# Turning the 128 x 1024 matrix C: identity products on TensorE, or 32 x 32 blocks on VectorE and transfers within SBUF

## The chip, the cores and the metric

The kernel runs on one core of a Trainium2 chip. The metric is the device time of one execution in microseconds (us); lower is better. All data are fp32. The traces were taken by the hardware profiler; times in a trace count from the start of its span.

## What is computed

Two layers, each a residual with a dense weight and a low-rank part that is picked per batch by a label:

```python
def _L0(x, labeler_index, W, lora_A, lora_B_w):
    base  = jnp.einsum('bsi,oi->bso', x, W)
    low   = jnp.einsum('bsi,bir->bsr', x, lora_A[labeler_index])       # rank 32, 5 labels
    return base + jnp.einsum('bsr,or->bso', low, lora_B_w) * 0.5

def _L1(x, adapter_mapping, W, b, lora_As, lora_Bs):
    base_out = jnp.einsum('bti,oi->bto', x, W) + b
    lora_h   = jnp.einsum('bti,bir->btr', x, lora_As[adapter_mapping]) # rank 16, 32 slots
    return base_out + jnp.einsum('btr,bro->bto', lora_h, lora_Bs[adapter_mapping]) * 2.0

x = x + _L0(x, itok_B_0_2, L0_W, L0_lora_A, L0_lora_B_w)      # x: (8, 256, 1024)
x = x + _L1(x, itok_B_0_23, L1_W, L1_b, L1_lora_As, L1_lora_Bs)
```

## The kernel before

**The dense part.** The two layers are folded into one matrix M = (I + W0)(I + W1), up to transposes. Stage 0 computes M, stages 1 and 2 multiply it by the two halves of x. Each stage is one multiplication of 2 x 2 blocks, done with seven block products instead of eight (`ORDER`), so there are 21 products, numbered n = 0 to 20; product 7 is the first of stage 1. Each operand is split into a high and a low part (`split`, L232): ScalarE writes the rounded high part (L234, tiles `arXh`, `brh`), VectorE the rest (L235, `arXl`, `brl`). A product is four output tiles (`tile(n, i)`, one PSUM bank each) of four steps k, and a step is three matmuls of 512 columns, so a product is 48 matmuls. `kept` (L333) takes a finished tile out of PSUM. Odd products read the ring half `ar1`, even ones `ar0`.

**The low-rank part and C.** What layer 1's down projections see is x after layer 0, so the kernel forms C, the gathered down projections (8 batches x 16 ranks = 128 rows) times I + W0, 128 rows by 1024 features. `across` makes C in two halves of 512 features, each in one PSUM bank: half 0 in bank `ps6` (done during product 1), half 1 in bank `ps7` (done at "sx", during product 3). The products of stages 1 and 2 need C with features in the partitions, as tile `ctile[128 features, 8, 128 rows]`, so each 128 x 128 block of C is turned. Before the change `ct_split` (L513) splits the half into `cth` (ScalarE, L515) and `ctl` (VectorE, L516), and `ct_turn` (L519) does eight matmuls of 128 columns with the identity `eye_r` (four blocks, high and low part), then ScalarE copies the bank to `ctile` (L526). Half 0 is turned between the first two tiles of product 2, half 1 before the last tile of product 3.

**Who reads ctile.** `load_a0(c)` (L628) splits 32 of the 128 rows for chunk c into `astk` (L234 on ScalarE, L235 on VectorE). `low_a` (L669) multiplies `astk` by x from the end of product 7 on; `low_rows` (L680) takes the result out into `pstk` (two ScalarE copies, a VectorE CAST at L688 and a VectorE subtraction at L689), and `low_f` (L695) is the next matmul on that bank, 18 matmuls after `low_a` ends. `pstk10` is the first of those tiles for chunk 1, in product 10.

**Memory.** `ct`, `a1hl`, `b0s` and others lie in the same bytes as the `keep` tiles of stages 1 and 2. Before, the first writers of those (L354, L364, L282 into `keep_w`) wait for the second turn, "tr 1".

**What sets the order.** The program is recorded as jobs with an assumed duration, and `rehearse` (L61) simulates five queues. PE keeps the order in which the code is written. On ScalarE, VectorE, GpSimd and the DMA-issuing SyncE a job is picked by the earliest start and then by its due time, which is worked backwards from the PE matmul that needs it. So a change of one job can move others on these four engines. Every engine runs its list in order, and a wait holds all that stands behind it. All DMAs are issued by SyncE (`transfer`, L190), one after another.

Of the kernel before, what the change touches and what calls it, by code (L numbers as in the profile page):

```python
# [6 lines left out]
ALU = mybir.AluOpType  # L7
# [114 lines left out]
def bass_blocks(nc, x, labels, w0, a0, b0, w1, bias, a1, b1, out):  # L122
    ctx = ExitStack()
    with ctx:
        def sb(name, shape, dt, where=None):
            return (where or ctx).enter_context(nc.sbuf_tensor(name, shape, dt))

        def sem(name):
            return ctx.enter_context(nc.semaphore(name))
# [12 lines left out]
        b0s = sb("b0s", [128, NK, 4, R], F32R, small)  # L142
        ct = [sb(f"ct{j}", [128, 512], F32R, small) for j in "hl"]
        b0raw = sb("b0raw", [128, NK, R], F32, small)
# [16 lines left out]
        eye = sb("eye", [128, 128], F32)  # L161
        eye_r = sb("eye_r", [128, 128], F32R)
        bias_t = sb("bias_t", [128, NO], F32)
# [6 lines left out]
        s_raw = [sem(f"s_raw{n}") for n in range(NRAW)]  # L170
        s_a1, s_b0, s_lab, s_bias = sem("s_a1"), sem("s_b0"), sem("s_lab"), sem("s_bias")
        counts, tokens, label = {}, {}, {}
        plan = Plan()

        def tk(*name):
            return tokens.setdefault(name, Token())
# [4 lines left out]
        def act(waits, emit, token, took):  # L181
            plan.put("act", waits, emit, token, took)

        def dve(waits, emit, token, took):
            plan.put("dve", waits, emit, token, took)
# [19 lines left out]
        def pe(out_ap, lhs, rhs, start, waits=(), name=None):  # L205
            n = 1
            for s in rhs.shape[1:]:
                n *= s
            plan.put("pe", waits, (out_ap, lhs, rhs, start), tk(*name) if name else Token(), max(n / 2400 + 0.0133, 0.107))
            plan.jobs[-1].named = bool(name)  # L210

        def take(bank):
            return bank_free.pop(bank, [])
# [7 lines left out]
            eye[:, :], ones[:, :], [[-1, 128]], ALU.is_equal, 0.0, base=0, channel_multiplier=1), tk("eye"), 0.4)  # L221
        act([tk("eye")], lambda e: e.activation(eye_r[:, :], eye[:, :], ACT.Copy), tk("eye_r"), 0.3)
        dve([], lambda e: e.memset(astk[:, :, :, 64:128].bitcast(F32), 0.0), tk("zero"), 0.9)
# [109 lines left out]
        def kept(n, i, done, half=None):  # L333
# [18 lines left out]
            if p == 0:  # L352
                spare = {0: [], 1: [tk("tr", 1)], 2: [tk("stored", 1, "s1", i, 0, 1)] if stage == 2 else []}[stage]
                act([done] + spare, lambda e: e.activation(s1, z, ACT.Copy), token, 0.65)  # L354
# [7 lines left out]
            elif p == 2:  # L362
                spare = {0: [], 1: [tk("tr", 1)], 2: [tk("stored", 1, "s5", i, 1, 1)] if stage == 2 else []}[stage]
                act([done] + spare, lambda e: e.activation(s5, z, ACT.Copy), token, 0.65)  # L364
# [17 lines left out]
            else:  # L382
# [7 lines left out]
                bank_free[bank] = [token]  # L390

        where["s1", 0], where["s5", 0], where["w", 0] = mb["11"], mb["22"], mb["12"]
        for s in (1, 2):
# [22 lines left out]
        def sum_t1(stage, groups=PAIRS):  # L416
            old = {0: lambda k: [], 1: lambda k: [tk("tr", 1)], 2: lambda k: [tk("stored", 1, "w", k, 1, 0)]}[stage]
            combine(stage, "T1", "B12", "B11", ALU.subtract, where["w", stage], old, groups)
# [93 lines left out]

        def ct_split(bank, done, half):  # L513
            spare = [tk("tr", 0)] if half else []
            act([done] + spare, lambda e: e.activation(ct[0][:, :], ps[bank][:, :], ACT.Copy), tk("ct_h", half), 0.65)  # L515
            dve([tk("ct_h", half)], lambda e: e.tensor_tensor(ct[1][:, :], ps[bank][:, :], ct[0][:, :].bitcast(F32), ALU.subtract), tk("ct_l", half), 0.72)  # L516
            bank_free[bank] = [tk("ct_l", half)]

        def ct_turn(bank, half):  # L519

            for i in range(4):
                for j in range(2):
                    pe(ps[bank][:, 128 * i:128 * i + 128], ct[j][:, 128 * i:128 * i + 128], eye_r[:, :], j == 0,
                       (take(bank) if i == 0 and j == 0 else []) + [tk("ct_h", half), tk("ct_l", half), tk("eye_r")],
                       ("tr", half) if (i, j) == (3, 1) else None)
            act([tk("tr", half)], lambda e: e.activation(  # L526
                ctile[:, 4 * half:4 * half + 4, :], ps[bank][:, :].rearrange("p (k r) -> p k r", k=4), ACT.Copy), tk("ctile", half), 0.65)
            bank_free[bank] = [tk("ctile", half)]

# [30 lines left out]
        four_rows(dtmp[2][:, :], dstk[:, 0:512], tk("sum", "d", 0), ("d", 0))  # L560
        ct_split(Y[2], tk("ct", 0, 1), 0)

# [8 lines left out]
        tile(2, 0, True)  # L571
        ct_turn(Y[2], 0)
        tile(2, 1, True)
# [12 lines left out]
        side_across((2, 3))  # L586
        ct_split(Y[3], tk("sx", 3), 1)
        tile(3, 1, True)
# [5 lines left out]
        tile(3, 2, True)  # L594
        ct_turn(Y[3], 1)
        tile(3, 3, True)
# [362 lines left out]
```

How the kernel before makes its waits and increments, by code:

```python
def wait_all(eng, waits, done):  # L115
    for t in waits:
        if done.get(t.sem, 0) < t.value:
            done[t.sem] = t.value
            eng.wait_ge(t.sem, t.value)
# [72 lines left out]
            def emit(eng):  # L192
                for i in numbers:
                    if i not in label:
                        label[i] = eng.value_load(label_t[:, i:i + 1], min_val=0, max_val=top)
                for dst, src in pairs():
                    eng.dma_start(dst, src).then_inc(s, 16)
# [683 lines left out]
        def run(eng, name, s):  # L881
            done = {}
            for job in order[name]:
                wait_all(eng, job.waits, done)
                job.emit(eng).then_inc(s, 1)
# [3 lines left out]
            @block.sync  # L889
            def _(eng):
                done = {}
                for job in order["sp"]:
                    wait_all(eng, job.waits, done)
                    job.emit(eng)
                for s in s_keep.values():
                    eng.wait_ge(s, counts[s])
# [13 lines left out]
            @block.tensor  # L910
            def _(eng):
                done = {}
                wait_all(eng, [tk("fzero")], done)
                zeros = fstk[:, 0, :]
                for i in range(WARM):
                    ins = eng.matmul(ps[7][:, :], zeros, zeros.unsqueeze(1).to_broadcast([128, 4, 128]), start=True, stop=True)
                ins.then_inc(s_pe, 1)
                for job in tensor:
                    wait_all(eng, job.waits, done)
                    out_ap, lhs, rhs, first = job.emit
```

## Time and profile before

| | |
|---|---|
| median of 3 runs | 291.45 us (291.11 to 291.81) |
| the profiled execution | 291.58 us |
| its span, first to last instruction | 289.9 us |
| PE busy | 285.6 us, 99% |
| VectorE (DVE) busy | 224.0 us, 77% |
| ScalarE (ACT) busy | 144.1 us, 50% |
| mean granted TensorE clock | 0.999 |

The profiled execution has 1.68 us outside its span. A matmul's busy time overlaps that of the next, so the pace of PE is read from the starts of matmuls, not from their durations. PE is TensorE's matmuls, PEld its weight loads, SPq the queue of SyncE that issues DMAs.

### The profile page before, as it was taken

The page shows a single profiled execution, that of the slowest core. Times are in us where ns is not written, and L with a number is a line of the kernel's source. Part 1 is how long each engine was busy: PE and PEld are TensorE (multiplying, and loading weights), DVE is VectorE, ACT ScalarE, POOL GpSimd, SP SyncE. Part 2 cuts the span into 40 slices and gives each one's busy share as a digit, 9 for nine tenths or more (in the row PEclk, how much of TensorE's full clock was granted, in tenths as well). Part 3 has the DMA queues.
Part 4 walks back from the last instruction along what each step waited for, and adds up shares of the span by engine and source line. Part 5 has one row for each costly group of instructions (what it writes and reads, how often), then busy time and mean ns, then how long its engine had stood idle before and what let it go on. Part 6 is the DMA issues. An engine that isn't in the chain of part 4 may idle for free.

```text
span 289.9 us, 3654 instructions
## 1 busy us (share of the span) xinstructions
PE 285.6 (99%) x1332; PEld 238.6 (82%) x1332; DVE 224.0 (77%) x266; ACT 144.1 (50%) x194; POOL 4.0 (1%) x13
## 2 busy tenths in 40 slices
PE   8999999999999999999999999999999999999995
PEld 5888788888888888888888888888988888888885
DVE  5967999898999989999885999838385956787400
ACT  4875457625367573836473540646565373505021
POOL 0000020000000000000000000000010000000000
PEclk9999999999999999999999999999999999999999
DMA  7959600212443010117241537330102100012222
GB/s 233 362 166 351 214 0 2 83 63 72 150 140 133 14 38 5 32 42 250 73 145 39 181 103 259 111 109 37 36 0 82 65 2 0 0 72 104 80 104 78
DMA packets 18628, 29.21 MB, mean 101 GB/s; under 512 B 2994, under 2 KB 5426, under 8 KB 18610
## 3 DMA queue, kind: packets, MB, share of 16 engines
q1 hardware_dynamic: 18610, 28.98, 29.9%
q8 instruction: 10, 0.16, 0.2%
q14 instruction: 8, 0.07, 0.1%
HBM read 20.58 MB, written 8.39 MB: 100 GB/s over the span
## 4 chain that ended last, share of the span: by engine, by line
PE 97%; DMA 1%; ACT 0%; DVE 0%; issue 0%
PE ps L921 97%; DMA w_B<-in_w 1%; ACT ar0h L234 0%; ACT brh L234 0%; DVE keep_s L735 0%; DVE w_B L441 0%
## 5 line engine op out<-in xcount | busy, mean ns | idle before, releaser
L921 PE MATMUL ps<-brh,ar0h 128*128 128x512 f32 (+1 forms) x180 | 68.9, 389 | 0.1
L921 PE MATMUL ps<-brl,ar0h 128*128 128x512 f32 (+1 forms) x180 | 68.3, 385 | 0.0
L921 PE MATMUL ps<-brh,ar0l 128*128 128x512 f32 (+1 forms) x180 | 68.2, 384 | 0.0
L234 ACT ACTIVATE brh<-w_B 128x1024 fp32r<-128x1024 f32 (+1 forms) x40 | 38.8, 969 | 57.8 <-PE ps L921 49.7
L921 PE MATMUL ps<-brh,ar1h 128*128 128x512 f32 x160 | 62.5, 391 | 0.0
L921 PE MATMUL ps<-brl,ar1h 128*128 128x512 f32 x160 | 62.4, 390 | 0.0
L921 PE MATMUL ps<-brh,ar1l 128*128 128x512 f32 x160 | 62.3, 389 | 0.0
L235 DVE TENSOR_TENSOR brl<-w_B,brh 128x1024 fp32r<-128x1024 f32 (+1 forms) x40 | 44.5, 1112 | 18.5 <-ACT brh L234 18.2
L921 PEld LDWEIGHTS ps<-brh,ar0h 128*128 128x128 f32 x180 | 34.1, 190 | 7.4 <-ACT ar0h L234 0.8
L921 PEld LDWEIGHTS ps<-brh,ar0l 128*128 128x128 f32 x180 | 33.8, 188 | 6.8
L921 PEld LDWEIGHTS ps<-brl,ar0h 128*128 128x128 f32 x180 | 33.9, 188 | 6.5
L921 PEld LDWEIGHTS ps<-brh,ar1h 128*128 128x128 f32 x160 | 30.1, 188 | 6.3 <-DVE m L343 0.3
L921 PEld LDWEIGHTS ps<-brh,ar1l 128*128 128x128 f32 x160 | 30.0, 188 | 6.3
L921 PEld LDWEIGHTS ps<-brl,ar1h 128*128 128x128 f32 x160 | 30.1, 188 | 5.9
L235 DVE TENSOR_TENSOR ar0l<-w_A,ar0h 128x1024 fp32r<-128x1024 f32 (+1 forms) x16 | 17.3, 1086 | 0.7 <-ACT ar0h L234 0.5
L345 DVE SCALAR_TENSOR_TENSOR keep_s<-ps,bias_t,keep_s 128x512 f32<-128x512 f32 x16 | 11.6, 745 | 6.9 <-PE ps L921 6.9
L234 ACT ACTIVATE ar0h<-w_A 128x1024 fp32r<-128x1024 f32 (+1 forms) x16 | 15.0, 944 | 1.5 <-DVE w_A L282 1.2
L387 ACT ACTIVATE keep_s<-ps,bias_t 128x512 f32<-128x512 f32 x7 | 4.8, 687 | 21.3 <-PE ps L921 21.3
L235 DVE TENSOR_TENSOR ar1l<-w_A,ar1h 128x1024 fp32r<-128x1024 f32 (+1 forms) x14 | 14.8, 1064 | 0.7 <-ACT ar1h L234 0.5
L282 DVE TENSOR_TENSOR w_B<-w_B 128x1024 f32<-128x1024 f32 x12 | 14.4, 1219 | 0.2
L234 ACT ACTIVATE ar1h<-w_A 128x1024 fp32r<-128x1024 f32 (+1 forms) x14 | 12.9, 927 | 0.6 <-PE ps L921 0.5
L921 PE MATMUL ps<-pstk,dstk 128*128 128x512 f32 x32 | 12.4, 389 | 0.0
(109 smaller groups left out, 348.6 us busy)
## 6 DMA issues: line engine op xcount, KB each, us to landing
w_B<-in_x SPq DMA_DIRECT2D x32, 256.0 KB, 2.9
out_z<-keep_s SPq DMA_DIRECT2D x23, 256.0 KB, 2.0
w_B<-in_w SPq DMA_DIRECT2D x16, 256.0 KB, 5.7
w_A<-in_w SPq DMA_DIRECT2D x16, 256.0 KB, 5.3
raw<-in_b SPq DMA_DIRECT2D x64, 32.0 KB, 1.7
out_z<-keep_w SPq DMA_DIRECT2D x8, 256.0 KB, 2.1
raw<-in_a SPq DMA_DIRECT2D x8, 128.0 KB, 2.8
a1raw<-in_a SPq DMA_DIRECT2D x8, 64.0 KB, 1.9
```

The costliest lines, as they stand in the source:

```text
L234: act(waits + spare, lambda e: e.activation(hi, src, ACT.Copy, scale=scale), h, 0.2 + 0.43 * wide)
L235: dve([h], lambda e: e.tensor_tensor(lo, src, hi.bitcast(F32), ALU.subtract), l, 0.15 + 0.54 * wide)
L282: lambda e, part=part, ins=ins: e.tensor_tensor(place[:, part, :], ins[0], ins[1], op),
L345: dve(waits + [tk("bias")], lambda e: e.scalar_tensor_tensor(out=dst, in0=z, scalar=bias_t[:, 4 * a + i:4 * a + i + 1], in1=other, op0=ALU ...
L387: act([done, tk("bias"), tk("stored", stage, "s1", i, 0, 0)], lambda e: e.activation(s1, z, ACT.Identity, bias=bias_t[:, 4 + i:5 + i]), to ...
L921: ins = eng.matmul(out_ap, lhs, rhs, start=first, stop=False, skip_group_check=True)
```

## The change

C is no longer split and multiplied by the identity. VectorE's transpose reads the half's PSUM bank and writes tile `ct[half]`, in which each 32 x 32 block is turned in its own place. The blocks then have to change places within the 128 partitions: SyncE issues 16 transfers from SBUF to SBUF for each half, one for each pair of source and target group of 32 partitions, of 32 partitions x 4 x 32 elements of 4 bytes. The first writers of the shared bytes now wait for both halves of `ctile` and two more tokens.

```diff
-        ct = [sb(f"ct{j}", [128, 512], F32R, small) for j in "hl"]
+        ct = [sb(f"ct{h}", [128, 512], F32, small) for h in range(2)]
-        eye_r = sb("eye_r", [128, 128], F32R)
-        act([tk("eye")], lambda e: e.activation(eye_r[:, :], eye[:, :], ACT.Copy), tk("eye_r"), 0.3)
...
+        small_done = [tk("ctile", 0), tk("ctile", 1), tk("dn", 3), tk("sum", "d2")]
...
-                spare = {0: [], 1: [tk("tr", 1)], 2: [tk("stored", 1, "s1", i, 0, 1)] if stage == 2 else []}[stage]
+                spare = {0: [], 1: small_done, 2: [tk("stored", 1, "s1", i, 0, 1)] if stage == 2 else []}[stage]
...
-        def ct_split(bank, done, half):
-            spare = [tk("tr", 0)] if half else []
-            act([done] + spare, lambda e: e.activation(ct[0][:, :], ps[bank][:, :], ACT.Copy), tk("ct_h", half), 0.65)
-            dve([tk("ct_h", half)], lambda e: e.tensor_tensor(ct[1][:, :], ps[bank][:, :], ct[0][:, :].bitcast(F32), ALU.subtract), tk("ct_l", half), 0.72)
-            bank_free[bank] = [tk("ct_l", half)]
-        def ct_turn(bank, half):
-            for i in range(4):
-                for j in range(2):
-                    pe(ps[bank][:, 128 * i:128 * i + 128], ct[j][:, 128 * i:128 * i + 128], eye_r[:, :], j == 0,
-                       (take(bank) if i == 0 and j == 0 else []) + [tk("ct_h", half), tk("ct_l", half), tk("eye_r")],
-                       ("tr", half) if (i, j) == (3, 1) else None)
-            act([tk("tr", half)], lambda e: e.activation(
-                ctile[:, 4 * half:4 * half + 4, :], ps[bank][:, :].rearrange("p (k r) -> p k r", k=4), ACT.Copy), tk("ctile", half), 0.65)
-            bank_free[bank] = [tk("ctile", half)]
+        def ct_turn(bank, done, half):
+            dve([done], lambda e: e.transpose(ct[half][:, :], ps[bank][:, :]), tk("blocks", half), 0.72)
+            bank_free[bank] = [tk("blocks", half)]
+            views = [ct[half][32 * c:32 * c + 32, :].rearrange("p (k q r) -> p k q r", k=4, q=4) for c in range(4)]
+            transfer([tk("blocks", half)], lambda: [
+                (ctile[32 * q:32 * q + 32, 4 * half:4 * half + 4, 32 * c:32 * c + 32], views[c][:, :, q, :])
+                for c in range(4) for q in range(4)], s_ct[half], tk("ctile", half), 8, count=16)
...
-        ct_split(Y[2], tk("ct", 0, 1), 0)
+        ct_turn(Y[2], tk("ct", 0, 1), 0)
-        ct_turn(Y[2], 0)
-        ct_split(Y[3], tk("sx", 3), 1)
+        ct_turn(Y[3], tk("sx", 3), 1)
-        ct_turn(Y[3], 1)
```

The change also moves instructions, since `rehearse` orders four engines anew; PE's order is the old one less the 16 identity matmuls. Three places matter below. Line numbers of the kernel after are one to nine lower for the same statement.

SyncE, from the last small load of stage 0 to the loads of x for stage 1 (`w_B<-in_x`) and of layer 1's up projections (`raw<-in_b`). Before:

```order
66 L197 DMA bias_t<-in_bias 128x8
67 L197 DMA w_B<-in_x 128x512 x12
68 L197 ISA
69 L197 DMA raw<-in_b 16x512 x4
70 L197 ISA
71 L197 DMA raw<-in_b 16x512 x4
72 L197 DMA w_B<-in_x 128x512 x4
```

And after:

```order
66 L197 DMA bias_t<-in_bias 128x8
67 L197 DMA ctile<-ct 32x4x32 x16
68 L197 DMA w_B<-in_x 128x512 x12
69 L197 DMA ctile<-ct 32x4x32 x16
70 L197 DMA w_B<-in_x 128x512 x4
71 L197 ISA
72 L197 DMA raw<-in_b 16x512 x4
```

Half 0 is issued ahead of the twelve loads of x, half 1 between them and the last four.

ScalarE, from the high parts of product 6 (`w_B21`, `w_A22`) to those of product 7 (`w_B12`, `m_11`). Before, where both splits of `ctile` stood ten instructions earlier:

```order
L663 ACTIVATE bstk0<-raw1 128x512
L663 ACTIVATE bstk0<-raw0 128x512
L506 ACTIVATE dstk<-dtmp2 32x512 x2
L234 ACTIVATE brh<-w_B12 128x1024
L234 ACTIVATE ar1h<-m_11 128x4x256
```

And after:

```order
L654 ACTIVATE bstk0<-raw1 128x512
L500 ACTIVATE dtmp0<-ps6 32x512
L233 ACTIVATE astk<-ctile 128x8x16
L233 ACTIVATE brh<-w_B12 128x1024
L233 ACTIVATE astk<-ctile 128x8x16
L233 ACTIVATE ar1h<-m_11 128x4x256
```

The first split of `ctile`, which waits for both halves' transfers, now stands directly ahead of the high parts of product 7.

VectorE, in product 10, around the rows `pstk10` that `low_f` waits for. Before:

```order
L282 TENSOR_TENSOR w_B22<-w_B22,w_B11 128x1024
L235 TENSOR_TENSOR brl<-w_B11,brh 128x1024
L235 TENSOR_TENSOR ar1l<-w_A11,ar1h 128x4x256
L688 CAST pstk10<-ps2 32x512
L235 TENSOR_TENSOR brl<-w_B11,brh 128x1024
L689 TENSOR_TENSOR pstk10<-ps2,pstk10 32x512
```

And after:

```order
L281 TENSOR_TENSOR w_B22<-w_B22,w_B11 128x1024
L234 TENSOR_TENSOR brl<-w_B11,brh 128x1024
L679 CAST pstk10<-ps2 32x512
L234 TENSOR_TENSOR ar1l<-w_A11,ar1h 128x4x256
L234 TENSOR_TENSOR brl<-w_B11,brh 128x1024
L680 TENSOR_TENSOR pstk10<-ps2,pstk10 32x512
```

Two long subtractions now stand between the CAST and the subtraction that completes `pstk10`, where one stood.

## Rows read from the trace of the kernel before

**Rows 1.** The page: busy us (share of the span), instructions; two rows in 40 slices.
```profile
PE 285.6 (99%) x1332; PEld 238.6 (82%) x1332; DVE 224.0 (77%) x266; ACT 144.1 (50%) x194; POOL 4.0 (1%) x13
PE   8999999999999999999999999999999999999995
PEclk9999999999999999999999999999999999999999
```

**Rows 2.** The chain that ended last: start us, us, what.
```profile
0.82 2.69 DMA w_B<-in_w
...
5.16 281.80 PE ps L921 x1324
...
286.99 0.42 DVE keep_s L735
```

**Rows 3.** The timeline of PE, first turn: start us, us, engine, line, operation.
```profile
40.54 0.22 PE L921 MATMUL ps<-eye_r,cth 128*128 128x128 f32 x1
...
41.38 0.45 PE L921 MATMUL ps<-brh,ar0h 128*128 128x512 f32 x1
...
44.22 0.39 PE L921 MATMUL ps<-ar0h,a1hl 128*128 128x512 f32 x1
```

**Rows 4.** The same, second turn, and the first matmuls of products 6 and 7.
```profile
66.88 0.22 PE L921 MATMUL ps<-eye_r,cth 128*128 128x128 f32 x1
...
67.72 0.45 PE L921 MATMUL ps<-brh,ar1h 128*128 128x512 f32 x1
...
70.56 0.39 PE L921 MATMUL ps<-brh,ar0h 128*128 128x512 f32 x1
...
92.32 0.39 PE L921 MATMUL ps<-brh,ar0h 128*128 128x512 f32 x1
...
103.20 0.39 PE L921 MATMUL ps<-brh,ar1h 128*128 128x512 f32 x1
```

**Rows 5.** The groups of instructions that write cth and ctl.
```profile
L515 ACT ACTIVATE cth<-ps x2: 598/599/600, 29.6 to 59.8; 128x512 fp32r<-128x512 f32 x2
L516 DVE TENSOR_TENSOR ctl<-ps,cth x2: 677/684/690, 36.5 to 60.5; 128x512 fp32r<-128x512 f32 x2
```

**Rows 6.** The timeline of VectorE near the end of product 4, and before product 7.
```profile
77.40 1.21 DVE L282 TENSOR_TENSOR w_B<-w_B 128x1024 f32<-128x1024 f32 x1
...
97.09 1.22 DVE L235 TENSOR_TENSOR ar1l<-m,ar1h 128x1024 fp32r<-128x1024 f32 x1
```

**Rows 7.** The timeline of SyncE's queue: issues of DMAs.
```profile
33.86 0.41 SPq L197 DMA_DIRECT2D bias_t<-in_bias  x1
53.21 26.24 SPq L197 DMA_DIRECT2D w_B<-in_x  x12
81.22 3.62 SPq L197 DMA_DIRECT2D raw<-in_b  x8
84.88 2.13 SPq L197 DMA_DIRECT2D w_B<-in_x  x4
```

**Rows 8.** Transfers: packets and share of 16 engines; issues, KB each, median us to landing.
```profile
q1 hardware_dynamic: 18610, 28.98, 29.9%
...
w_B<-in_x SPq DMA_DIRECT2D x32, 256.0 KB, 2.9
...
raw<-in_b SPq DMA_DIRECT2D x64, 32.0 KB, 1.7
```

**Rows 9.** The timeline of ScalarE, high part of product 7's operand.
```profile
91.24 1.06 ACT L234 ACTIVATE brh<-w_B 128x1024 fp32r<-128x1024 f32 x1 [0.61 <-PE ps L921]
```

**Rows 10.** The timeline of all engines in product 10, around pstk10.
```profile
145.42 0.40 PE L921 MATMUL ps<-brl,astk 128*128 128x256 f32 x2
...
145.53 1.22 DVE L235 TENSOR_TENSOR ar1l<-w_A,ar1h 128x1024 fp32r<-128x1024 f32 x1 [0.54 <-ACT ar1h L234]
...
146.78 0.69 DVE L688 CAST pstk<-ps 32x512 fp32r<-32x512 f32 x1
...
148.76 0.68 DVE L689 TENSOR_TENSOR pstk<-ps,pstk 32x512 fp32r<-32x512 f32 x1
...
149.67 0.30 PEld L921 LDWEIGHTS ps<-pstk,fstk 128*128 128x128 f32 x2 [0.16 <-issue]
149.77 0.40 PE L921 MATMUL ps<-pstk,fstk 128*128 128x256 f32 x2
...
150.21 0.59 ACT L686 ACTIVATE pstk<-ps 32x512 fp32r<-32x512 f32 x1 [0.69 <-PE ps L921]
```

More of the change, by code:

```diff
@@ L171, in bass_blocks @@
         s_a1, s_b0, s_lab, s_bias = sem("s_a1"), sem("s_b0"), sem("s_lab"), sem("s_bias")
+        s_ct = [sem(f"s_ct{h}") for h in range(2)]
         counts, tokens, label = {}, {}, {}
@@ L362, in kept @@
             elif p == 2:
-                spare = {0: [], 1: [tk("tr", 1)], 2: [tk("stored", 1, "s5", i, 1, 1)] if stage == 2 else []}[stage]
+                spare = {0: [], 1: small_done, 2: [tk("stored", 1, "s5", i, 1, 1)] if stage == 2 else []}[stage]
                 act([done] + spare, lambda e: e.activation(s5, z, ACT.Copy), token, 0.65)
@@ L416, in sum_t1 @@
         def sum_t1(stage, groups=PAIRS):
-            old = {0: lambda k: [], 1: lambda k: [tk("tr", 1)], 2: lambda k: [tk("stored", 1, "w", k, 1, 0)]}[stage]
+            old = {0: lambda k: [], 1: lambda k: small_done, 2: lambda k: [tk("stored", 1, "w", k, 1, 0)]}[stage]
             combine(stage, "T1", "B12", "B11", ALU.subtract, where["w", stage], old, groups)
```

## The prediction

> **What bounds the kernel now.** I read the page first. TensorE is busy for 99% of the span and full in every slice but the first and the last, at the full granted clock throughout, while VectorE has 77% and ScalarE 50% [rows 1]. The chain of waits says the same more strictly: after 5.16 us of start-up it is one piece of 281.80 us on PE with 1324 matmuls, and only the last 0.4 us are VectorE's [rows 2]. So the end is set by how many matmuls PE issues and at what pace, and anything else counts only if it makes PE wait. Next I read the pace, from starts of matmuls. Product 6 begins at 92.32 and product 7 at 103.20 [rows 4]: 48 matmuls of 512 columns in 10.88 us, 0.2267 us each. That is the yardstick for what the identity products cost. Last I looked at what stands near the new steps on VectorE, ScalarE and SyncE's queue, to find how late C may come [rows 6 to 10].
>
> **What goes from PE.** Each turn is eight matmuls of 128 columns. In the first turn they start at 40.54 and the next real product at 41.38, 0.84 us. But that product is slowed too: the twelve matmuls of its tile last until 44.22 [rows 3]. From 40.54 to 44.22 are 3.68 us, and twelve at the yardstick are 12 x 0.2267 = 2.72, so the turn costs 0.96 us. The second turn: from 66.88 to 70.56 again 3.68 us with twelve product matmuls in it [rows 4], again 0.96. Both stand in the unbroken PE piece, so both are on the path: 2 x 0.96 = **1.92 us** to gain. The lower bound of the gain, if the slow tile after the turn has another cause, is 2 x 0.84 = 1.68 us.
>
> **What speaks against it in the notes.** The row shows 0.96 us for four blocks of 128 x 128 in two parts, all of it on the engine that bounds. The Trainium skill (VectorE: DVE Perf Modes, Rules for kernel authors) says to turn 128 x 128 on TensorE where PSUM may be the destination, and its table of the three transpose paths gives 390 ns on TensorE for one such block of bf16 and 311 ns on VectorE for one that is turned only within 32 x 32 blocks. By its figures the estimate for eight blocks is 3.1 us on TensorE instead of the 1.92 that the rows give, and the gain would be larger than I take. The rule looks at the engine's own time, and here the row decides.
>
> **What goes from and comes to VectorE and ScalarE.** ScalarE loses two writes of `cth` at 0.598 us [rows 5], two copies to `ctile` and `eye_r`; at 50% it gives nothing to the path. VectorE loses two subtractions of 0.684 us and gets two transposes of the same 128 x 512 from PSUM. No row shows a transpose. Nearest are the subtraction at 0.684 [rows 5] and, above, an instruction of twice the elements, 1.22 [rows 6]. A gain is excluded, since both read the same bank once at one column after another. I take 0.69, the same size. At 1.22 each, 0.5 us more stands ahead of work with some us of cover: nothing on the path.
>
> **Half 0 on SyncE.** C's first half is in PSUM by 29.6, and VectorE subtracts at 36.5 [rows 5], where the transpose stands now, so it is turned by 37.2. SyncE has nothing to issue from 34.3 to 53.21 [rows 7]. Sixteen issues fit: the eight small loads `raw<-in_b` took 3.62 us [rows 7], 0.45 us each, so 7.2 us, to about 44.5. Cost nothing; the cover is 8 us. PE's `down` on the same bank now waits for the transpose alone, earlier than before.
>
> **Half 1, the step that could bite.** All times here are on the clock of the trace; with PE 1.9 us ahead most of them move together. VectorE turns half 1 only after the subtraction that starts at 77.40 and ends at 78.6 [rows 6], although C is there at 59.8 [rows 5]. Turned by 79.3. SyncE then issues 16 transfers of 0.45 us, to 86.5. Landing takes 1.7 us for small loads and 2.9 for loads of x [rows 8], so C is complete between 88.2 and 89.4. The engines set a second limit. A transfer of 32 x 4 x 32 elements is 128 runs of 128 bytes, so a half is 2048, or 128 on each of 16 engines. The page has 18610 packets in 29.9% of 16 engines' span [rows 8]: 0.299 x 16 x 289.9 / 18610 = 0.0745 us each. 128 of these are 9.5 us, and C would be complete at 79.3 + 9.5 + 1.7 = 90.5. So the bounds are 88.2 and 90.5, and I take 89.4, as the mean packet is much larger than 128 bytes.
>
> Who waits: ScalarE's first split of `ctile` now stands directly ahead of `brh` for product 7, which ran at 91.24 and waited for PE then [rows 9]. With C by 90.5 and 0.3 us for the split, it isn't even moved. If it were, there is more cover. The last low part of product 7 was ready at 97.09 + 1.22 = 98.3 [rows 6], and PE takes it at the third step, six matmuls after 103.20 [rows 4], at 104.56: 6.2 us. VectorE's split of `ctile` stands ahead of the copy of product 5's last bank, which product 6 wants only at its last tile, 36 matmuls after 92.32: no less cover. So PE waits only if C is complete later than 91.24 + 6.2 - 0.3 = 97.1. Behind the 16 issues on SyncE stand the last four loads of x (84.88 before, about 86.6 now) and `raw<-in_b`, 81.22 before and about 88.7 now [rows 7]. The first are operands of product 8 and later; the latter's low-rank matmuls come after product 7. Both have over 10 us: nothing.
>
> **The moved VectorE step in product 10.** `low_a` for chunk 1 issues its last matmul at 145.54, the second of the pair at 145.42, and a reader starts 0.32 us after such a matmul (149.89 to 150.21) [rows 10]. Now the CAST is taken at 145.86, `ar1l` 0.72 later (146.58), `brl` 1.14 later (147.72) and the subtraction 1.26 later (148.98), against 148.76 before; it ends 0.68 later at 149.66. PE loads these weights at 149.67 and multiplies at 149.77 [rows 10], so the cover of 0.22 us is just used up. I put **0.1 us**, with 0 and 0.3 as ends. Around product 8 the same swap has over a microsecond left by the same counting.
>
> **Sum.** On the profiled execution: 291.58 - 1.92 + 0.1 = 289.76. The median of the runs is 0.13 below it, so I forecast 291.45 - 1.92 + 0.1 = 289.6 us. Its own range is 289.3 (the full gain and some noise) to 290.0 (1.68 gained and 0.3 lost).
>
> **Rivals.** (1) *VectorE hands part back.* VectorE's list is reordered over products 2 to 10, and PE now asks 1.9 us sooner. For it: the thin 0.22 us in product 10, and others I may have missed. Against: PE's piece of the chain is unbroken [rows 2], and the covers are microseconds elsewhere. Two or three such stalls of 0.3 us give 290.3.
>
> (2) *The gain does not show.* If some supplier runs on its own time from 67 us on, PE just waits 1.9 us once. For it: loads of x are issued one after another, 32 issues more. Against: all products' operands wait for PE's release of the ring, and so move with it. It would give 291.4.
>
> (3) *The transfers are slow, and it is slower than before.* The mechanism is half 1's small packets holding ScalarE's queue ahead of product 7's high parts. It decides from a completion at 97.1, so from 17.8 us for the half, 1.1 us per transfer. If a 128-byte packet took twice the mean of the page, 0.149 us, 128 of them take 19.1 us and C is complete at 79.3 + 19.1 + 2.9 = 101.3. PE waits 4.2 us, and the time is 291.45 - 1.92 + 4.2 = 293.7 us. For it: such a packet is not in the trace. Against: the mean packet is 1.56 KB and takes 0.0745 us, and a smaller one should not take longer. The Trainium skill (DMA: Bandwidth & Descriptors, Specifications) puts the least transfer for line rate at 512 bytes and says that below it the engine reads, modifies and writes; this rival is that rule as a doubling. That the bytes per packet are small is certain; that the doubled time passes the cover is not.
>
> **How the numbers follow.** Forecast 0.72; VectorE hands back 0.12; no gain shows 0.09; slow transfers 0.07. A measurement of this kernel can tell about 0.2%, 0.58 us. Below 290.87 lie the forecast and the first rival: faster 0.84. Within 0.2% the second: 0.09. Slower 0.07. The range must leave out no more than 0.2: from 289.2 it reaches past the first rival, to 290.8, which holds 0.84.
>
> **What would show it.** PE should have 1316 matmuls, and go from tile to tile at 0.2267 us where the turns stood, with the starts of product 7 at about 101.3. Sixteen issues of 0.45 us should follow the transpose near 77.5 (79.3 less 1.9), with completion near 87.5, and ScalarE's split of `ctile` should wait for DMA by less than 2 us. A gap before the first `pstk`,`fstk` matmul of product 10 would show the small loss. The prediction is wrong if PE's rows show a wait for ScalarE or VectorE at the start of product 7, if one issue takes a microsecond, or if a transpose takes several.

## The result

| | before | after |
|---|---|---|
| median of 8 runs each, same chip | 291.48 us (291.11 to 292.03) | 290.50 us (290.29 to 291.31) |
| ratio to before, with its 95% interval | | 0.9968 (0.9957 to 0.998) |
| the profiled execution | 291.58 us | 290.38 us |
| its span | 289.9 us | 288.7 us |

The change makes the kernel 0.98 us faster, 0.3%. The forecast was 289.6 us, a gain of 1.85 us. The sign is right and 290.5 lies in the range, but half of the gain is missing. Five more runs of the changed kernel beside before on another chip gave 290.55 us and 0.9961 (0.9948 to 0.9973), so the missing half is no accident of one chip.

The page of after, in the same form as [rows 1]:

```profile
PE 283.7 (98%) x1316; PEld 236.3 (82%) x1316; DVE 223.3 (77%) x266; ACT 140.4 (49%) x189; POOL 2.9 (1%) x13
PE   7999999999999999999999999999999999999995
```

TensorE has 16 matmuls fewer, as it should, and seems as full as before. Nothing on this page says where 0.9 us went. The chain that ended last does (start us, us, what; before it was one unbroken piece of PE, [rows 2]):

```profile
34.80 79.32 PE ps L912 x356
114.19 1.06 ACT ar1h L233
...
119.62 0.69 DVE pstk L680
120.56 165.20 PE ps L912 x786
```

The chain leaves PE at 114.19, in product 8, and comes back at 120.56 by a VectorE instruction, L680, the subtraction that completes the rows `pstk`. So somewhere near 120 us PE waited for VectorE, which it didn't before.

**The bookkeeping by starts of matmuls.** The cleanest way to see where time comes and goes is to put the same matmul of both kernels side by side. The timeline of PE, before, at the last product matmul ahead of the first turn and at the tile in product 8 that takes `pstk` (start us, us, engine, line, operation):

```profile
40.32 0.39 PE L921 MATMUL ps<-brh,ar0l 128*128 128x512 f32 x1
...
121.81 0.39 PE L921 MATMUL ps<-brh,ar0l 128*128 128x512 f32 x1
122.04 0.40 PE L921 MATMUL ps<-pstk,fstk 128*128 128x256 f32 x2
```

And after, at the turns' places, then at the same tile, then at its fellow in product 10:

```profile
40.14 0.39 PE L912 MATMUL ps<-brh,ar0l 128*128 128x512 f32 x1
40.37 0.39 PE L912 MATMUL ps<-brh,ar0h 128*128 128x512 f32 x1
...
65.75 0.39 PE L912 MATMUL ps<-brh,ar1h 128*128 128x512 f32 x1
...
119.73 0.39 PE L912 MATMUL ps<-brh,ar0l 128*128 128x512 f32 x1
120.56 0.48 PE L912 MATMUL ps<-pstk,fstk 128*128 128x256 f32 x2 [0.44 <-DVE pstk L680]
120.87 0.40 PE L912 MATMUL ps<-brh,ar0h 128*128 128x512 f32 x1
...
148.12 0.39 PE L912 MATMUL ps<-brh,ar0l 128*128 128x512 f32 x1
148.49 0.48 PE L912 MATMUL ps<-pstk,fstk 128*128 128x256 f32 x2
148.80 0.39 PE L912 MATMUL ps<-brh,ar0h 128*128 128x512 f32 x1
```

The product tile behind the first turn started at 41.38 before [rows 3] and starts at 40.37 now, 1.01 earlier; that behind the second at 67.72 [rows 4] against 65.75, 1.97 earlier. Just ahead of `pstk` the two stand at 121.81 and 119.73: 2.08 earlier. Not all of that is the turns': the last product matmul ahead of the first turn stands at 40.32 and 40.14, 0.18 earlier already, since PE's small waits before 36 us came out shorter in this execution. The two turns together brought 2.08 - 0.18 = 1.90. Then comes the step from 119.73 to 120.56, 0.83 us where before had 0.23. That is 0.60 lost, and the next matmul starts 0.31 later instead of 0.23, 0.08 more. In product 10 the same two steps are 0.37 and 0.31 where before had 0.23 (149.54 to 149.77) and 0.24: 0.21 more. 2.08 - 0.68 - 0.21 = 1.19, and the spans differ by 1.2. Nothing else on the path moved. Without the 0.18 it would be 1.01, and the medians differ by 0.98.

The idle time printed beside the matmul, 0.44, is smaller than the 0.60 by the starts, since a matmul's busy time overlaps the next one's. The gap is read from starts.

### The profile page after: what moved, and what is told of

Read it like the earlier page. It is cut to its first block, busy times and chain, and to the rows that moved or that the text cites. A ratio compares the mean times of both kernels' runs of the same rounds, so it can differ in the third digit from the quotient of the medians.

```text
span 288.7 us, 3652 instructions
## 1 busy us (share of the span) xinstructions
PE 283.7 (98%) x1316; PEld 236.3 (82%) x1316; DVE 223.3 (77%) x266; ACT 140.4 (49%) x189; POOL 2.9 (1%) x13
## 2 busy tenths in 40 slices
DMA packets 23236, 29.74 MB, mean 103 GB/s; under 512 B 7602, under 2 KB 10034, under 8 KB 23218
## 3 DMA queue, kind: packets, MB, share of 16 engines
q1 hardware_dynamic: 23218, 29.51, 31.3%
## 4 chain that ended last, share of the span: by engine, by line
PE 85%; SPq 7%; DMA 2%; ACT 2%; DVE 2%; issue 1%; DVEq 0%; ACTq 0%
PE ps L912 85%; SPq L197 6%; DMA w_A<-in_w 2%; SPq L195 1%; ACT ar1h L233 1%; DVE w_A L281 0%; DVE brl L234 0%; DVE ar0l L234 0%; ACT brh L233 0%; ACT astk L233 0%; DVE pstk L680 0%; DVE m L342 0%; ACT pstk L678 0%; ACT keep_s L353 0%; ACT pstk L677 0%
## 5 line engine op out<-in xcount | busy, mean ns | idle before, releaser
L344 DVE SCALAR_TENSOR_TENSOR keep_s<-ps,bias_t,keep_s 128x512 f32<-128x512 f32 x16 | 11.6, 747 | 6.7 <-PE ps L912 6.6
```

The lines of the kernel that those rows point to most:

```text
L344: dve(waits + [tk("bias")], lambda e: e.scalar_tensor_tensor(out=dst, in0=z, scalar=bias_t[:, 4 * a + i:4 * a + i + 1], in1=other, op0=ALU ...
```

## Why VectorE was late at 119.62: reading back

Two things had changed for VectorE, and both lie ahead of that subtraction. First the order. These are the rows of VectorE before, in product 8:

```profile
118.63 0.69 DVE L688 CAST pstk<-ps 32x512 fp32r<-32x512 f32 x1
119.47 0.68 DVE L689 TENSOR_TENSOR pstk<-ps,pstk 32x512 fp32r<-32x512 f32 x1 [0.16 <-ACT pstk L687]
```

And after:

```profile
117.64 0.69 DVE L679 CAST pstk<-ps 32x512 fp32r<-32x512 f32 x1
118.36 1.22 DVE L234 TENSOR_TENSOR brl<-keep_w,brh 128x1024 fp32r<-128x1024 f32 x1
119.62 0.68 DVE L680 TENSOR_TENSOR pstk<-ps,pstk 32x512 fp32r<-32x512 f32 x1
```

A long subtraction of 1.22 us, a low part for product 9, now stands between the CAST and the step that PE waits for. It is the swap that the prediction costed in product 10. Second, VectorE had come late to this place. The queue of SyncE in after, against [rows 7], and behind it what waits for it on ScalarE and VectorE:

```profile
37.32 10.43 SPq L197 DMA_DIRECT2D ctile<-ct  x16
52.55 27.48 SPq L197 DMA_DIRECT2D w_B<-in_x  x12
80.08 10.25 SPq L197 DMA_DIRECT2D ctile<-ct  x16
90.37 2.02 SPq L197 DMA_DIRECT2D w_B<-in_x  x4
```

```profile
91.63 0.31 ACT L233 ACTIVATE astk<-ctile 128x128 fp32r<-128x128 f32 x1 [4.18 <-DMA ctile<-ct]
...
91.97 0.29 DVE L234 TENSOR_TENSOR astk<-ctile,astk 128x128 fp32r<-128x128 f32 x1 [2.98 <-ACT astk L233]
```

Sixteen issues take 10.25 us, 0.64 each, not 7.2. They also begin late, at 80.08 and not near 77.5. VectorE shows why:

```profile
76.84 0.69 DVE L342 TENSOR_TENSOR m<-ps,m 128x512 f32<-128x512 f32 x1 [0.49 <-PE ps L912]
77.44 1.22 DVE L281 TENSOR_TENSOR w_B<-w_B 128x1024 f32<-128x1024 f32 x1
78.58 0.71 DVE L516 STREAM_TRANSPOSE ct<-ps 128x512 f32<-128x512 f32 x1
```

The subtraction `w_B<-w_B` ahead of the transpose starts at 77.44, and in before at 77.40 [rows 6]: it didn't come earlier with PE, since in the new order it stands behind a copy of a bank that waits for PE, which in before ran behind it, at 78.92. And on SyncE the last two of the twelve loads of x, for which this subtraction makes room, are issued ahead of half 1, until 80.03. So C is complete at 91.6, 1.3 us after the last issue ends, ScalarE's first split of `ctile` waits 4.18 us and VectorE's 2.98 us behind it. From 91.97 to 119.62, over 27 us, VectorE has no wait in its rows: it works off what queued up. In before it still had small waits there, 0.32 us at the low part ahead of the CAST among them. So the 2.98 us are partly still there 27 us later; the experiments show 1.09 of them.

A number that helps from here on is the **cover** of `pstk` in product 8. In after the subtraction starts at 119.62 and PE's matmul at 120.56, 0.94 later, and PE wanted to start it at 119.73 + 0.23 = 119.96. The cover is what is left between the moment at which the subtraction should start at the latest (PE's wanted start less 0.94) and the start it has. In before it is 122.04 - 0.94 - 119.47 = 1.63 us, in after 119.96 - 0.94 - 119.62 = -0.60: the gap.

## The experiments

**The theory**: the identity products were worth the full 1.9 us, and about 0.6 to 0.7 came back in product 8, by the swap and by the late C together. **The rivals**: the products were worth less than was read; the new order alone costs it; the slow 128-byte packets do. All kernels are the changed one or the one before with the edit shown. `shift(lane, job, ahead_of)` takes one job out of an engine's finished list and puts it ahead of another; `("B", 1, 9, 2)` is the low part of product 9's second operand, second half, and `("p", 1, 0, c)` the subtraction that completes `pstk` of chunk c.

**1. The products alone (e_no_turn).** The kernel before, with its 16 identity matmuls left out and all else in its old order. C isn't turned here: ScalarE copies it to `ctile` as it is, once the low part is written.

```diff
         order, tensor = plan.rehearse(5.0)
+        tensor = [job for job in tensor if job.emit[2].tensor.name != eye_r.name]
...
+        for half in range(2):
+            tk("tr", half).sem, tk("tr", half).value = s_dve, tk("ct_l", half).value
```

> The kernel before with the 16 identity matmuls taken off PE and nothing else changed: ScalarE copies C to ctile unturned, so C is not turned here and the low-rank part of layer 1 is computed from the wrong layout. It prices the first term alone. By the starts of matmuls the turns cost 2 x 0.96: 291.5 - 1.9 = 289.6 us. If the slower pace of the twelve matmuls behind a turn has another cause, only 2 x 0.84 goes: 289.8 us. If PE only waits elsewhere for what it gains, it stays near 290.5.

Measured: 289.76 us against 291.66, ratio 0.9935 (0.992 to 0.9951). That is 1.90 us for the products, against 1.92 by the prediction's count of [rows 3, 4], and no gap at `pstk`. The first rival falls: the term of the sum was right, the loss comes from the new parts.

**2. The order alone (e_before_swap).** The kernel before, with VectorE's list changed as in after: in product 8 the long subtraction ahead of the completing one, in product 10 the CAST ahead of `ar1l`.

```diff
+        shift("dve", ("B", 1, 9, 2), ("p", 1, 0, 0))
+        shift("dve", ("p", 3, 0, 1), ("A", 1, 11, 0))
```

> The kernel before, identity products and all, with VectorE's list changed only where the kernel after has it changed around pstk: in product 8 one brl ahead of the subtraction of pstk00, in product 10 the CAST ahead of ar1l. Theory L: in the kernel before VectorE is not behind, the subtraction of pstk00 ends 1.15 us later at 121.3 and PE wants it at 121.9, so no gap there; at most 0.2 us in product 10. Time 291.5 to 291.7 us. Rival O: PE loses 0.6 us at pstk00 and 0.2 at pstk10, 292.3 us.

Measured: 291.67 us against 291.66, ratio 1.0002 (0.999 to 1.0014). In product 8 the step stays at 0.22 us (121.73 to 121.95). The subtraction starts at 120.52, so the cover went from 1.63 to 121.95 - 0.94 - 120.52 = 0.49 us, and it holds. The swap alone isn't enough. In product 10 the gap is there: 149.46 to 149.83, 0.37 us, just as in after, so that small one is the order's alone. Its 0.2 us are too few to be seen in the medians.

**3. C early (e_early).** The changed kernel, with half 1's transpose and its 16 transfers moved ahead, ahead of a low part of product 4 and of loads of x.

```diff
+        shift("dve", ("blocks", 1), ("A", 1, 4, 2))
+        shift("sp", ("ctile", 1), ("f", 1, "B12", 0))
```

> The kernel after, with two moves and nothing else: VectorE's transpose of half 1 stands ahead of the last low part of product 4 (about 60 us) and SyncE's 16 transfers ahead of the loads of w_B11, so C is complete some 20 us earlier. The two moved steps of pstk in products 8 and 10 stay as in the kernel after. Theory L (late C): the kernel after loses 0.6 us at the first pstk,fstk matmul (119.73 to 120.56) because C is complete only at about 91.6, ScalarE waits 4.2 us for it, VectorE 3.0 us for ScalarE, and VectorE is still behind in product 8. Then here ScalarE's wait for C is gone, the subtraction of pstk00 ends near 119.2, PE goes through at 0.23 us, and the time is 290.5 - 0.7 = 289.8 us. Rival O (order alone): the swap on VectorE's list costs the 0.6 us by itself; then PE's gap stays at 0.8 us between starts and the time stays at 290.5.

Measured: 289.73 us against 291.66, ratio 0.9933 (0.9919 to 0.9947). The interval lies below that of after. Rows of SyncE, ScalarE, VectorE and PE in it:

```profile
60.81 10.25 SPq L197 DMA_DIRECT2D ctile<-ct  x16
```

```profile
87.23 0.29 ACT L233 ACTIVATE astk<-ctile 128x128 fp32r<-128x128 f32 x1
...
113.81 1.23 DVE L234 TENSOR_TENSOR brl<-keep_w,brh 128x1024 fp32r<-128x1024 f32 x1 [0.32 <-ACT brh L233]
...
118.38 0.68 DVE L680 TENSOR_TENSOR pstk<-ps,pstk 32x512 fp32r<-32x512 f32 x1
...
119.59 0.39 PE L921 MATMUL ps<-brh,ar0l 128*128 128x512 f32 x1
119.81 0.40 PE L921 MATMUL ps<-pstk,fstk 128*128 128x256 f32 x2
```

The issues are just as slow, but nobody waits for them. VectorE again has its 0.32 us of slack ahead of the low part, which shows that it isn't working off a queue. The completing subtraction starts 1.24 us sooner than in after, the cover is 119.81 - 0.94 - 118.38 = 0.49, and the gap is gone. The swap is still in there.

**4. The order put back (e_rows_first).** The changed kernel, C as late as in after, but both completing subtractions ahead of the long one, as in before.

```diff
+        shift("dve", ("p", 1, 0, 0), ("B", 1, 9, 2))
+        shift("dve", ("p", 1, 0, 1), ("B", 1, 11, 2))
```

> The kernel after, with VectorE's two subtractions that complete pstk00 and pstk10 each put ahead of the low part of brl that stood before it; C stays late. Both theories expect the gaps on PE to go: 0.69 us at product 8 and 0.19 us at product 10, so 290.5 - 0.9 = 289.6 us. It tells whether the two gaps are the whole of what is missing. If some of the missing gain lies elsewhere (in the operands of products 9 and 11, which come 0.7 us later here), the time stays above 290.

Measured: 289.72 us against 291.66, ratio 0.9932 (0.9917 to 0.9947). The subtraction starts at 118.43 and PE goes on at 120.01 to 120.23, without a gap; product 10 has none either. So each of the two causes is needed: take away the late C or the swap, and the gap is gone.

**5. Both (e_both), with the changed kernel again (e_after_again).** The four `shift` lines of 3 and 4 together.

> The kernel after with both cures: half 1 turned and moved early as in e_early, and the two subtractions of pstk ahead of brl as in e_rows_first. Theory L: nothing of the 1.92 us is handed back, no gap on PE at either pstk,fstk; about 0.2 us under e_early and the same as e_rows_first or 0.1 under it: 1.95 us below the kernel before, 0.9 to 1.0 below the kernel after. Rival: the cures share the same 0.7 us and nothing is added: the same as e_early.

> The kernel after, unchanged, beside the three below on one chip, as their base: 290.5 us, with the gap of 0.8 us between starts ahead of pstk,fstk in product 8 in its trace.

Measured: 289.79 us and 0.9929 (0.9916 to 0.9941) for both edits, 290.55 and 0.9961 for the changed kernel. The cover is back at 1.62 us, where before has 1.63, but cover beyond what is needed gives no more time, as the rival of the expectation had it: 3, 4 and 5 can't be told apart (their intervals overlap almost wholly), and all are 0.7% below before. A repair of either kind is worth 0.8 us, a little more than the 0.68 counted in product 8. The rest is of the size of PE's small waits before 36 us, which vary between executions; at a gap near 34 us, where PE waits for VectorE's copy L342 during product 1, by up to 0.5 us. The step between the starts of its two matmuls is 0.29 us in before, 0.50 in after, 0.59 in e_both and 0.79 in e_double (experiment 7).

**6. Is it the number of issues, or the late transpose (e_one_transfer)?** One transfer of 128 x 512 for each half in place of 16; the blocks don't change places. The last line leaves `rehearse` the duration that it assumed for sixteen, so the order stays that of after; the same line stands in 7 and 8.

```diff
-            views = [ct[half][32 * c:32 * c + 32, :].rearrange("p (k q r) -> p k q r", k=4, q=4) for c in range(4)]
-            transfer([tk("blocks", half)], lambda: [
-                (ctile[32 * q:32 * q + 32, 4 * half:4 * half + 4, 32 * c:32 * c + 32], views[c][:, :, q, :])
-                for c in range(4) for q in range(4)], s_ct[half], tk("ctile", half), 8, count=16)
+            one = ct[half][:, :].rearrange("p (k r) -> p k r", k=4)
+            transfer([tk("blocks", half)], lambda: [(ctile[:, 4 * half:4 * half + 4, :], one)], s_ct[half], tk("ctile", half), 8)
+            plan.jobs[-1].took = 0.45 * 16
```

> The kernel after with the 16 transfers of each half replaced by one of 128 x 512 elements; the instruction order of all engines is otherwise that of the kernel after. The 32 x 32 blocks are not exchanged here, so the low-rank part of layer 1 is computed from wrong positions. Theory L with the issue time as its cause: one issue takes about 0.45 us and C is complete at 80.1 + 0.45 + 2 = 82.5, before ScalarE asks for it at 87.4; its wait and VectorE's go, the gap in product 8 goes, 0.2 us in product 10 stays: 0.7 us below the kernel after. Rival: the late transpose, not the number of issues, is what makes VectorE late; then the time stays that of the kernel after.

Measured: 289.71 us against 291.8, ratio 0.9937 (0.9922 to 0.9952). The transfer is issued at 80.41, no sooner than the first of the sixteen in after (80.08), ScalarE's split runs at 88.24 with no wait, and product 8 has no gap (cover 0.50). So the place of the transpose, 79.45 here and 78.58 in after, doesn't hurt by itself, and neither do issues of 0.64 us by themselves (experiment 3); late start and slow issues together do. This kernel has fewer small packets as well as fewer issues. What parts the two is that in after the packets keep up with the issues: C is complete 1.3 us after the last of them ends. The interval lies below that of after in the first table, 0.9957 to 0.998, but overlaps that of after on this chip, 0.9948 to 0.9973, a little; the rows of the trace are the stronger evidence.

**7. How the delay is handed on (e_four_more, e_double).** Ahead of half 1's 16 transfers stand four more of the same shape, and in the second kernel sixteen more (there `range(4)` in both cases), all into a tile not yet in use.

```diff
+            again = [pstk[1][1][:, :].bitcast(F32).rearrange("p (k r) -> p k r", k=4), ctile[:, 4:8, :]] if half else [ctile[:, 0:4, :]]
...
-                for c in range(4) for q in range(4)], s_ct[half], tk("ctile", half), 8, count=16)
+                for place in again for c in range(4) for q in (range(4) if place is again[-1] else range(1))], s_ct[half], tk("ctile", half), 8, count=16 + 4 * half)
```

> The kernel after with four more transfers of the same shape ahead of half 1's 16, to a tile that is not read; same order. C is complete 4 x 0.64 = 2.6 us later, at about 94.2. Theory L says that the gap at pstk,fstk in product 8 is VectorE's backlog and grows by the whole delay, since VectorE has no idle time between the wait for C and that subtraction: from 0.6 to 3.2 us beyond PE's pace, while the copy of product 5's last bank, at 95.4, is still ahead of the last tile of product 6, which asks for it near 98.5, so no wait there. The time is 2.6 us above the kernel after, 1.6 us above the kernel before (plus what TensorE's clock costs, if it falls after a gap of 3 us). By the cover of the prediction (C no later than 95.0 on this clock) nothing would change.

Measured, four more: 294.03 us against 291.57, ratio 1.0091 (1.0066 to 1.0116). The profiled execution took 293.0. Its rows on ScalarE, VectorE and PE:

```profile
94.25 0.31 ACT L233 ACTIVATE astk<-ctile 128x128 fp32r<-128x128 f32 x1 [6.35 <-DMA ctile<-ct]
...
122.25 0.68 DVE L682 TENSOR_TENSOR pstk<-ps,pstk 32x512 fp32r<-32x512 f32 x1
...
120.17 0.39 PE L914 MATMUL ps<-brh,ar0l 128*128 128x512 f32 x1
123.19 0.47 PE L914 MATMUL ps<-pstk,fstk 128*128 128x256 f32 x2 [2.63 <-DVE pstk L682]
```

C comes 94.25 - 91.63 = 2.62 us later than in after, and the subtraction 122.25 - 119.62 = 2.63 later. Once VectorE has no slack left, a microsecond of delay at 92 us is a microsecond at 120 us. The gap is 3.02 - 0.23 = 2.79 us and not the 3.2 expected, because PE itself stood 0.44 later in this execution (120.17 against 119.73, from its waits before 36 us); 2.79 + 0.44 is 2.63 more than after's 0.60. The profiled time is 2.6 above after, as expected. The median is 1 us more than that, since two of the four runs have a span 1.0 to 1.7 us longer than the other two, and a mean granted clock of 0.994. When in these two the clock was lower isn't shown, as they have no trace. The next kernel shows a lower clock in its rows.

> The kernel after with half 1's 16 transfers issued twice, first to a tile that nothing reads, then to ctile; same order. It moves C's completion from 91.6 to 80.1 + 2 x 10.25 + 1.8 = 102.4 and tests the cover that the prediction gave, a completion at 97.1 on the clock of the kernel before, 95.0 on this one. If that cover is right PE waits about 7.4 us ahead of the third step of product 7 and the time is 7 to 7.5 us above the kernel after (the gap in product 8 may change by some tenths). If VectorE's backlog reaches PE elsewhere first, more than 8 us; if the cover is larger, less.

Measured, sixteen more: 302.13 us against 291.8, ratio 1.0354 (1.0334 to 1.0373), 11.6 above after. I had expected 7 to 7.5, and more than 8 only if VectorE's backlog reached PE elsewhere first, which is what happened. The profiled execution took 300.78, 10.4 above that of after. C is complete at 101.98, 102.4 was expected. PE, at the last tile of product 6:

```profile
98.46 0.39 PE L914 MATMUL ps<-brh,ar0l 128*128 128x512 f32 x1
103.86 0.80 PE L914 MATMUL ps<-brh,ar0h 128*128 128x512 f32 x1 [5.01 <-DVE m L342]
104.45 0.63 PE L914 MATMUL ps<-brl,ar0h 128*128 128x512 f32 x1
104.88 0.63 PE L914 MATMUL ps<-brh,ar0l 128*128 128x512 f32 x1
```

And busy times by stretch (window, us, PE, PEld, DVE, ACT, POOL busy, granted clock, DMA share, GB/s):

```profile
98.50:103.80 5.30, 0.35 (x2) 0.00 (x0) 1.48 (x4) 1.82 (x4) 0.00 (x0) 0.94 0.45 114
103.90:110.00 6.10, 6.10 (x14) 4.75 (x15) 6.01 (x7) 6.00 (x10) 0.00 (x0) 0.50 0.39 125
110.00:118.00 8.00, 8.00 (x38) 6.62 (x37) 7.99 (x8) 6.26 (x10) 0.00 (x0) 1.00 0.17 36
```

PE waits 5.40 - 0.23 = 5.17 us, for VectorE's copy L342 of a bank, not for the operands of product 7. From the wait's last 0.7 us on the granted clock is 0.50, the 1.2 GHz level, until 110.00, with matmuls 0.43 us apart: 14 of them in 6.14 us in place of 3.17, 3.0 lost. At `pstk` in product 8 VectorE is then 129.97 - 119.62 = 10.35 us later than in after and PE 128.22 - 119.73 = 8.49, so the gap should be 0.60 + 10.35 - 8.49 = 2.46; the step is from 128.22 to 130.91, 2.69 - 0.23 = 2.46. What my expectation had missed is the clock, which takes 3.0 us, the gap in product 8, which grows by 1.86, and that the bank's wait comes ahead of the operands'. 5.17 + 3.0 + 1.86 = 10.0 of the 10.4 us of the profiled execution; PE's waits before 36 us have 0.3 more. Three of the five runs took 1.2 to 1.8 us longer than the other two; why isn't shown.

**8. What sets 0.64 us (e_shapes2).** Half 0 goes by 18 transfers of six shapes; only the issues in the trace are read.

```diff
+                pairs = [(other[:, :, 32 * c:32 * c + 32], whole[:, :, 32 * c:32 * c + 32]) for c in range(4)]
+                pairs += [(here[0:32, :, 32 * c:32 * c + 32], whole[0:32, :, 32 * c:32 * c + 32]) for c in range(4)]
+                pairs += [(here[32:64, k, :], whole[32:64, k, :]) for k in range(4)]
+                pairs += [(here[64:96, k, 0:32], whole[64:96, k, 0:32]) for k in range(4)]
+                pairs += [(here[64:96, :, 32:128], whole[64:96, :, 32:128])]
+                pairs += [(here[96:128, :, :], whole[96:128, :, :])]
```

`here` is half 0's part of `ctile`, `whole` is `ct[0]` seen as 128 x 4 x 128, and `other` is a tile of `pstk` not yet in use. The four of the first line have 512 runs of 128 bytes each, those of the third and fourth 32 runs.

> The kernel after with half 0's 16 transfers replaced by transfers of different shapes from ct to ctile or to an unread tile, in this order: four of 128 x 4 x 32 elements (512 runs of 128 bytes), four of 32 x 4 x 32 (128 runs of 128 bytes, as in the kernel after), four of 32 x 128 (32 runs of 512 bytes), four of 32 x 32 (32 runs of 128 bytes), one of 32 x 4 x 96 (128 runs of 384 bytes), one of 32 x 512 (32 runs of 2048 bytes). Half 0 of C is not turned correctly here. The prediction took 0.45 us for an issue from small loads of 16 runs; the kernel after takes 0.64. If the number of runs sets the issue time, the shapes order as 512 runs over 128 over 32, the first well above 0.64 and both shapes of 32 runs at 0.4 or under. If the third dimension of the access sets it, 512 and 128 runs cost the same 0.64 and the two-dimensional ones 0.45. If the source in SBUF sets it, all take 0.64.

Issues by form in it (count, ns shortest/median/longest, from when to when):

```profile
L197 SPq DMA_DIRECT2D ctile<-ct x30: 587/601/710, 40.2 to 90.0; - x30
L197 SPq DMA_DIRECT2D pstk<-ct x4: 627/640/747, 37.4 to 39.5; - x4
L197 SPq DMA_DIRECT2D out_z<-keep_s x25: 332/333/818, 131.7 to 286.6; - x25
```

And in before:

```profile
L197 SPq DMA_DIRECT2D raw<-in_b x64: 316/369/1312, 29.8 to 191.9; - x64
L197 SPq DMA_DIRECT2D w_B<-in_x x32: 327/426/455, 53.2 to 177.0; - x32
```

Shape and number of runs matter little: leaving out the first of a kind, an issue within SBUF takes 0.59 to 0.60 us with 32 runs, 0.60 to 0.63 with 128 and 0.63 to 0.64 with 512, and 0.04 passes until the next. That holds for issues in a row; the two lone transfers of experiment 6 took 0.54 and 0.88, and the load of x right ahead of half 1's row in after 0.98. Loads from memory have medians of 0.37 and 0.43, stores to it 0.33. What the slow ones have in common is that both ends lie in SBUF. Why that is dearer no run shows.

**All covers side by side**, in product 8, each from the starts of the subtraction and of PE's matmul in that kernel's trace. In all three kernels with a gap the matmul starts 0.94 us after the subtraction.

| kernel | swap | ScalarE's split of C at | cover of `pstk`, us | gap on PE, us |
|---|---|---|---|---|
| before | no | | 1.63 | 0 |
| before with the swap | yes | | 0.49 | 0 |
| C early | yes | 87.23 | 0.49 | 0 |
| one transfer | yes | 88.24 | 0.50 | 0 |
| **after** | yes | 91.63 | -0.60 | 0.60 |
| four more | yes | 94.25 | -2.79 | 2.79 |
| sixteen more | yes | 101.98 | -2.46 | 2.46 (after 8.2 us lost in product 6) |
| late C, rows first | no | 91.69 | 0.86 | 0 |
| both edits | no | 88.19 | 1.62 | 0 |

The swap takes 1.14 us of the cover, the late C 1.09 more (in the kernel with the rows first PE itself was 0.27 us later, by a gap near 34 us, so its 0.86 is 0.59 on after's clock, close to 1.63 - 1.09). By the one-to-one handing on of experiment 7 the gap would be nil with the split at 91.63 - 0.60 = 91.0 or sooner, an estimate.

## Where the prediction was right and where it failed

**What bounds, and what goes from PE: right.** 1.92 us were forecast; without the products alone the kernel has 1.90 less, and in the changed kernel PE gains 1.90 between the first turn and product 8's gap. The slowed tile behind a turn does belong to the turn's price: the starts at the yardstick give it, and it was paid back.

**The transpose: right.** 0.70 and 0.71 us for the two, against 0.69.

**Half 0: right in cost, by its cover.** 10.43 us in place of 7.2, between 37.3 and 52.55 on an idle SyncE.

**Half 1, the first step that failed: when C is complete.** The prediction had 87.5 on after's clock, measured are 91.6. Two of its terms were too small, one too large. *The price of an issue.* The prediction took 0.45 us, from eight loads `raw<-in_b` in 3.62 us [rows 7]. The kind of transfer was another one, and the trace of before has none within SBUF. Measured are 0.64 us, 10.25 for the half, 3.05 more. Since the price was unmeasured, its range should have been opened upward; the bounds were set only for the landing and the packets. *The start.* "With PE 1.9 us ahead most of them move together" didn't hold for the subtraction ahead of the turn (77.44 against 77.40), and the loads of x still before half 1 on SyncE weren't counted: the issues began at 80.08 and not at 77.4, 2.7 later. *The landing* took 2.9 us in the prediction; C was complete 1.3 us after the last issue's end, 1.6 less. 87.5 + 3.05 + 2.7 - 1.6 = 91.6. By the estimate of 91.0 for the last harmless completion either of the first two alone would have passed: 88.6 with the right price, 89.0 with the right start.

The packets were no matter: 23218 after against 18610, with a share of 31.3% against 29.9% [rows 8], are (0.313 x 288.7 - 0.299 x 289.9) x 16 / 4608 = 0.013 us each, far below the mean of 0.0745, and a landing takes 1.8 us (median). The Trainium skill (DMA: Bandwidth & Descriptors, Why small descriptors are slow (HBM only)) says that transfers between SBUF and SBUF don't suffer the penalty for small descriptors; the packets of this trace agree, with their 0.013 us, and the rule of 512 bytes that stood behind the third rival doesn't show here.

**Half 1, the second step that failed: who waits.** "PE waits only if C is complete later than 97.1." The count looked at the two consumers that come right behind, product 7's operands and the last bank of product 5, and each did have the cover stated: PE goes through product 7 without a gap. It left out that the wait sits on VectorE's own list, and that this list has little slack between 92 and 120 us: before's rows there show waits of 0.78, 0.32 and 0.16 us. Of the wait of 2.98 us 1.09 came out 27 us later, at the first step for which PE waits closely, and took more than the cover left there. In after's clock the point from which it costs is 91.0, not 97.1 - 2.0 = 95.1. The doubled kernel shows the bank of product 5 as the next consumer to run dry, and four more don't reach it.

**Product 8, the third: "the same swap has over a microsecond left".** Measured with the swap alone: 0.49 us. Before had 1.63 and the long subtraction takes 1.14. Alone this cover would have held, and with a correct completion of C beside it the loss could have been seen: 0.49 - 1.09.

**Product 10: right.** Forecast 0.1 (0 to 0.3), measured 0.21 by the starts, twice the middle and inside the bounds, by the mechanism named; it appears in before too when the swap is made there.

**The rivals.** The first, VectorE hands part back, is what happened, at 0.89 us in two places where it was priced at two or three times 0.3. Of its mechanism the new order is half of the cause; PE asking sooner costs nothing by itself, as PE does so without the products too and has no gap there. That the stated range holds 290.5 is owed to this rival, whose stalls were guessed and not located: the working's own range, 289.3 to 290.0, doesn't hold it. The second doesn't hold, as the 1.90 show. The third had the right waiter, ScalarE's split ahead of product 7's high parts, but the wrong cause, since the issues were slow and not the packets, and PE then waited in product 8 and not in product 7.

**The sum with what was measured**: 291.58 - 0.18 (ahead already before the first turn) - 1.90 (the turns) + 0.68 (product 8) + 0.21 (product 10) = 290.39, against 290.38 profiled.

## What to carry to other kernels

A wait on a busy in-order engine isn't paid where it stands: follow it down that engine's list, counting its slack, to the first step for which the bounding engine waits closely, and compare it with the cover left there. When work moves from the bounding engine into many small transfers, price their issue by a transfer of the same kind, both ends in the same memories; if the trace has none, open the range upward. Here either repair, issuing the transfers 20 us earlier or putting the completing subtraction first, brings back 0.8 us and gives 289.7 us, 0.7% below before. And when a step is said to move with the bounding engine, look at what stands ahead of it in the new order.

## What the runs showed of the hardware that was not expected

- In a row of issues on SyncE's queue one takes 0.59 to 0.64 us when source and target are both in SBUF, from 32 to 512 runs, against medians of 0.37 and 0.43 for loads and 0.33 for stores.
- In a PE wait of 5.17 us the granted clock fell to 0.50, the 1.2 GHz level, stayed there for the 6.1 us of matmuls behind the wait and then was 1.00 again, which cost 3.0 us on top. With four more transfers, where the traced execution has a wait of 2.79 us at a clock of 1.0, the mean clock was 0.994 in two of four runs.
- Eight identity matmuls of 128 columns cost 0.96 us of PE, of which 0.12 lay in the slower pace of the twelve large matmuls behind them; all of it came back when they went.
